# LayerNorm's small operations between statistics and power: from VectorE to GpSimd, in two-operand form

## The chip, the cores and the metric

The kernel runs on one core of a Trainium2 chip. The metric is the device time of one execution in microseconds (us). Three runs of the kernel before gave 407.63, 406.25 and 405.65 us; their median is 406.25 us. The engines are PE (TensorE, matmuls), DVE (VectorE), ACT (ScalarE), POOL (GpSimd) and SP (SyncE, which only issues transfers here).

## What is computed

There are 16 batches (B) of 512 tokens (T) with 256 features (D), and a context of 64 rows (K) per batch. Two cross-attentions follow each other.

```
layer 0:  q = rmsnorm(x) Wq^T, 16 heads of 16;  k, v from rmsnorm(ctx)
          token t looks at the context rows idx[t]-1, idx[t], idx[t]+1 only
          w = relu(q.k / 4)^2, divided by max(sum w, 1e-6);  x' = x + (w v) Wo^T
layer 1:  q = gelu(x' Wq + bq), k, v = gelu(ctx W + b), one head
          y = softmax(q k^T) v Wf + bf + x'
          out = (y - mean(y)) * rsqrt(var(y) + 1e-5) * gamma + beta     over the 256 features
```

The change concerns the last line alone. VectorE's `bn_stats` gives for every row of y the mean and the sum of squared deviations (m2) of its even and of its odd elements. With these, mean = (mean_e + mean_o) / 2 and var = (m2_e + m2_o) / D + (mean_e - mean_o)^2 / 4.

## The kernel before

All of it is written by hand: five instruction streams, one for each engine, with semaphores. Nothing is planned by a scheduler, and each stream is in order.

After a prologue for the weights and the context, a software pipeline runs over the batches. `steps` calls, for every engine, `step(f, b, n)`: the layer-0 attention of batch f, the layer-1 queries and softmax of batch b = f-1, and the end of batch n = f-2 (value product, LayerNorm, output). There is a step (0, -, -), a step (1, 0, -), then the steps from f=2 to f=14, the step of f=15 (`last`, in which no next batch is prepared), the step (-, 15, 14) and the step (-, -, 15). VectorE's step is cut in a `head` and a `tail` (`steps_turned`).

What stands around the change in a step, by engine and line:

- TensorE: picked keys (L388, a matmul with a one-hot matrix as look-up); L465, which adds the values of batch n to y in PSUM and signals `z_mm`; the output projection of b (L346 to L348); the first half of the next batch's layer-0 query product (L346 to L348, weight q0); the head sums (L495), which need the third key product (`qk_ready`) and signal `s_mm`; the second half of the query product; four transposes of the scores (L513), which need `s_cp`; the layer-1 queries of b (L346, weight q1), which need `xp_hi` and `xp_lo`; picked values (L394), which need `zn_ready` for the bank they write; then the turning of the attention output (L414), scores (L562, L570), and the softmax's transposes (L580).
- VectorE, `head`: two key products (L819), `bn_stats` of batch n (L834, four instructions, the last signals `stats_ready`), the six small operations (L839 to L846), the third key product (L819), the sum `xpT` (L861, from PSUM and the input), `xp_lo` (L864, from two SBUF tiles). `tail`: the row sum `den` (L883) and what follows from it, the three attention products (L870), the one-hot matrices, the softmax, `o_lo` (L927).
- GpSimd: `x_lo` of the next batch (L298), the power `rstd` = var^(-0.5) (L310), `nbias` = -mean * rstd (L313), then multiplication by gamma (L321), addition of beta (L323) and the output's transfer (L325).
- ScalarE: `normalise(range(0, 2))` (L666, y * rstd + nbias for two of the four row tiles; waits for `z_mm` and `nbias_ready`), `round_xp` (L687, `xp_hi`), the copy of the scores `s_sb` (L702, waits for `s_mm`), a copy of the next queries (L656), the square of the weights (L709, waits for TensorE's transposes), `normalise(range(2, 4))`, and the rest. In the step (-, 15, 14) `round_xp` stands ahead of the normalise. In the last step there is only the LayerNorm: statistics, power, normalise, gamma and beta on VectorE (L937, L939), output.

Of the kernel before, what the change touches and what calls it, by code (L numbers as in the profile page):

```python
# [5 lines left out]
B, T, D, K, H = 16, 512, 256, 64, 16  # L6
HD = D // H
P = 128
DC = D // P
TT = T // P  # L10
# [4 lines left out]
LN_EPS = 1e-05  # L15
# [7 lines left out]
def xattn_pair(nc: bass.Bass, xT, ctx, ctxT, idx, vectors, wq0T, wk0T, wv0T, wo0T,  # L23
# [4 lines left out]
    ALU = mybir.AluOpType  # L28
# [4 lines left out]
    with es:  # L33
        def sb(name, shape, dt=f32):
            return es.enter_context(nc.sbuf_tensor(name, shape, dt))
# [14 lines left out]
        minus_half = sb("minus_half", [P, CT])  # L50
# [39 lines left out]
        enf = sb("enf", [P, TT, K])  # L90
        eT = sb("eT", [P, 2, P])
        stats = sb("stats", [P, TT, 6])
        mean_gap, nmean2, m2_sum, gap_sq, var = (sb(n, [P, TT]) for n in ("mean_gap", "nmean2", "m2_sum", "gap_sq", "var"))
        rstd = sb("rstd", [P, TT])
        nmean = sb("nmean", [P, TT])
        nbias = sb("nbias", [P, TT])
        bufs = sb("bufs", [P, 8, DC * T])

# [5 lines left out]
        def rows(t):  # L104
# [38 lines left out]
        smax_ready, sdiff_ready, ex_ready, ssum_ready, rsum_ready, enf_ready = map(sem, (  # L143
            "smax_ready", "sdiff_ready", "ex_ready", "ssum_ready", "rsum_ready", "enf_ready"))
        eT_mm, eT_ready, z_mm = map(sem, ("eT_mm", "eT_ready", "z_mm"))
        stats_ready, parts_ready, gap_ready, var_ready, rstd_ready, nmean_ready, nbias_ready = map(sem, (
            "stats_ready", "parts_ready", "gap_ready", "var_ready", "rstd_ready", "nmean_ready", "nbias_ready"))
        zn_ready, zg_ready, zo_ready, out_done, last_zg, last_zo, last_out_done = map(sem, (
            "zn_ready", "zg_ready", "zo_ready", "out_done", "last_zg", "last_zo", "last_out_done"))

        def out_rows(j, at=0, cols=D):

            at += (j % 2) * D
            return ps[:, 6 + j // 2, at:at + cols]
# [12 lines left out]
        def steps(engine, step):  # L167
            step(0, None, None)
            step(1, 0, None)
            for i in range(FIRST_STEADY, LAST_STEADY):  # L170
                step(i, i - 1, i - 2)
            step(B - 1, B - 2, B - 3, last=True)
            step(None, B - 1, B - 2)
            step(None, None, B - 1)
# [17 lines left out]
        def first(n):  # L192
            return isinstance(n, int) and n == 0

        def is_last(n):
            return isinstance(n, int) and n == B - 1

        def f32_view(t):
            return t.bitcast(f32)
# [82 lines left out]
        @block.gpsimd  # L282
        def _(pool):
            G = nc.gpsimd
            G.memset(minus_half[:, :], -0.5).then_inc(half_set, 1)

            def context_scale(n):

                tiles = slice(4 * n, 4 * n + 4)
                pool.wait_ge(cms_done, 4 * n + 4)  # L290
                G.tensor_scalar(cmean[:, tiles], cms[:, tiles], 1.0 / D, EPS_RMS, ALU.mult, ALU.add).then_inc(cmean_done, 1)
                pool.wait_ge(cmean_done, n + 1)
                pool.wait_ge(half_set, 1)
                G.tensor_tensor(crs[:, tiles], cmean[:, tiles], minus_half[:, tiles], ALU.pow).then_inc(crs_done, 1)  # L294

            def split_x_lo(f):
                pool.wait_ge(xh_ready, 2 * f + 2)
                G.tensor_tensor(x_lo[:, :, :], x_ring[:, f % RING, :, :], f32_view(x_hi[:, :, :]), ALU.subtract).then_inc(xl_ready, 2)  # L298

            context_scale(0)  # L300
            split_x_lo(0)
            context_scale(1)

            def step(f, b, n, last=False):
                if f is not None and not last:
                    split_x_lo(f + 1)
                if n is not None:

                    pool.wait_ge(var_ready, n + 1)
                    G.tensor_tensor(rstd[:, :], var[:, :], minus_half[:, 0:TT], ALU.pow).then_inc(rstd_ready, 1)  # L310
                    pool.wait_ge(rstd_ready, n + 1)
                    pool.wait_ge(nmean_ready, n + 1)
                    G.tensor_tensor(nbias[:, :], nmean[:, :], rstd[:, :], ALU.mult).then_inc(nbias_ready, 1)  # L313
                if n is not None and not is_last(n):

                    pool.wait_ge(zn_ready, 2 * n + 2)
                    if first(n):
                        pool.wait_ge(ln_in, 16 * 2)
                    else:
                        pool.wait_ge(out_done, 16 * n)  # L320
                    G.tensor_tensor(zo, zn, lng_row[:, :].unsqueeze(1).broadcast_to([P, TT, D]), ALU.mult).then_inc(zg_ready, 1)  # L321
                    pool.wait_ge(zg_ready, n + 1)
                    G.tensor_tensor(zo, zo, lnb_row[:, :].unsqueeze(1).broadcast_to([P, TT, D]), ALU.add).then_inc(zo_ready, 1)  # L323
                    pool.wait_ge(zo_ready, n + 1)
                    pool.dma_start(out[n].rearrange("(j p) d -> p j d", p=P), zo).then_inc(out_done, 16)  # L325

            steps(pool, step)
            pool.wait_ge(out_done, 16 * (B - 1))

# [260 lines left out]
        def _(act):  # L590
# [79 lines left out]
            def step(f, b, n, last=False):  # L670
# [19 lines left out]
                    round_xp()  # L690
                if n is not None:
                    act.wait_ge(z_mm, n + 1)
                    act.wait_ge(nbias_ready, n + 1)
                    if not first(n):
                        act.wait_ge(zg_ready, n)
                    normalise(range(0, 2))
# [20 lines left out]
                if b is not None:  # L717
                    for e in range(DC):
# [3 lines left out]
                        i = A(q1T[:, e, :], ps[:, 2 + e, :], ACT.Gelu, bias=vec[:, 2, e:e + 1])  # L722
# [19 lines left out]
        def _(dve):  # L742
            V = nc.vector
# [77 lines left out]
            def head(f, b, n):  # L821
                if f is not None:
                    multiply_keys(f, 0, 4)
                    if first(f):
                        for t in range(4, 6):
                            keys_values_remainder(t)
                    multiply_keys(f, 1, 0)
                    if first(f):
                        for t in range(6, CT):
                            keys_values_remainder(t)  # L830
                if n is not None:
                    dve.wait_ge(z_mm, n + 1)
                    for j in range(TT):
                        i = V.bn_stats(stats[:, j, :], out_rows(j))  # L834
                    i.then_inc(stats_ready, 1)

                    dve.wait_ge(stats_ready, n + 1)
                    mean_e, m2_e, mean_o, m2_o = (stats[:, :, i] for i in (1, 2, 4, 5))
                    V.tensor_tensor(mean_gap[:, :], mean_e, mean_o, ALU.subtract)  # L839
                    V.scalar_tensor_tensor(nmean2[:, :], mean_e, -1.0, mean_o, ALU.mult, ALU.subtract)  # L840
                    V.scalar_tensor_tensor(m2_sum[:, :], m2_e, D * LN_EPS, m2_o, ALU.add, ALU.add).then_inc(parts_ready, 1)
                    dve.wait_ge(parts_ready, n + 1)
                    V.scalar_tensor_tensor(gap_sq[:, :], mean_gap[:, :], 0.25, mean_gap[:, :], ALU.mult, ALU.mult).then_inc(gap_ready, 1)
                    V.tensor_scalar(nmean[:, :], nmean2[:, :], 0.5, None, ALU.mult).then_inc(nmean_ready, 1)
                    dve.wait_ge(gap_ready, n + 1)
                    V.scalar_tensor_tensor(var[:, :], m2_sum[:, :], 1.0 / D, gap_sq[:, :], ALU.mult, ALU.add).then_inc(var_ready, 1)  # L846
                if f is not None:
                    multiply_keys(f, 2, 4)
                    if first(f):
                        dve.wait_ge(w1_in, 16 * 2)  # L850
                        for t in range(2, 6):
                            dve.wait_ge(kv_in[t], 32)
                        for i, name in enumerate(("o0", "q1")):
                            V.tensor_copy(w_hi[name][:, :, :], raw[name]).then_inc(w1_hi_ready, 1)
                            dve.wait_ge(w1_hi_ready, i + 1)
                            V.tensor_tensor(w_lo[name][:, :, :], raw[name], f32_view(w_hi[name][:, :, :]), ALU.subtract).then_inc(w1_ready, 1)
                if b is not None:

                    for g in range(DC):
                        dve.wait_ge(xp_mm, 2 * b + g + 1)  # L860
                        V.tensor_tensor(xpT[:, g, :], ps[:, 2 + g, :], x_ring[:, b % RING, g, :], ALU.add).then_inc(xp_ready, 1)  # L861
                    for g in range(DC):
                        dve.wait_ge(xph_ready, 2 * b + g + 1)
                        V.tensor_tensor(xp_lo[:, g, :], xpT[:, g, :], f32_view(xp_hi[:, g, :]), ALU.subtract).then_inc(xpl_ready, 1)  # L864
# [117 lines left out]
```

## Time and profile before

| | |
|---|---|
| median of 3 runs | 406.25 us (405.65 to 407.63) |
| profiled execution | 407.22 us, its span 405.4 us |
| mean granted TensorE clock | 0.98 |
| busy: PE, DVE, ACT, POOL | 91%, 76%, 57%, 37% of the span |
| one steady step (from one L298 on GpSimd to the next) | 209.88 to 231.13, 21.25 us |

The profile is of one execution. A line of the timeline is a run of like instructions with the time in which the engine stood idle before it and what ended that; "issue" there is a wait that the profile puts down to nothing. Busy time is an average over stages with different limits, so what a change is worth is read from the stage in which it stands. The profiled execution took 0.97 us more than the median.

### The profile page before, as it was taken

To read this page: it belongs to the slowest core of one execution; us is meant where nothing else is said; L and a number is where in the kernel's file an instruction comes from. 1 tells how busy PE (TensorE), PEld (TensorE's weight loads), DVE (VectorE), ACT (ScalarE), POOL (GpSimd) and SP (SyncE) were. 2 spreads that over 40 slices of the span, in tenths; PEclk is the share of its full clock that TensorE was granted. 3 is DMA by queue.
4 is the path that set the end of the run, shared out by engine and by line. 5 is a ranking of instruction groups with operands and counts; after the bars stand their busy time and mean duration, and the time that the engine had idled before them with its cause. 6 is when DMAs were issued, how large, how long until landed. Compare 5 with 4: busy or idle time off the path is not lost.

```text
span 405.4 us, 5734 instructions
## 1 busy us (share of the span) xinstructions
PE 370.7 (91%) x2132; PEld 262.5 (65%) x2132; DVE 306.2 (76%) x588; ACT 231.6 (57%) x379; POOL 148.8 (37%) x102
## 2 busy tenths in 40 slices
PE   3977999999999999999999999999999999998660
PEld 1653886858576776767676767676768576756540
DVE  0888266887979796969696969697978879797614
ACT  4793413557475656575656657474747474746441
POOL 0630002035353534434343525253535353515151
PEclk9998999999999999999999999999999999999985
DMA  8875056012011212121212121212121110010111
GB/s 253 282 214 158 0 128 159 0 54 64 32 72 43 78 53 78 53 79 54 78 54 78 53 78 53 78 52 81 52 77 54 41 68 25 0 53 11 41 53 52
DMA packets 17339, 30.24 MB, mean 75 GB/s; under 512 B 1568, under 2 KB 7712, under 8 KB 17312
## 3 DMA queue, kind: packets, MB, share of 16 engines
q1 hardware_dynamic: 14192, 21.22, 17.3%
q0 software_dynamic: 2160, 7.87, 5.5%
q10 hardware_dynamic: 960, 0.79, 0.6%
q8 instruction: 17, 0.28, 0.3%
q14 instruction: 10, 0.08, 0.1%
HBM read 17.29 MB, written 8.39 MB: 63 GB/s over the span
## 4 chain that ended last, share of the span: by engine, by line
PE 80%; issue 7%; ACT 5%; DVE 4%; POOL 3%; ACTq 0%; POOLq 0%; DVEq 0%
PE ps L346 11%; PE ps L348 10%; PE ps L347 10%; PE ps L414 10%; PE ps L495 7%; PE ps L394 7%; PE ps L388 6%; PE ps L465 4%; PE ps L562 4%; PE ps L550 3%; PE ps L513 2%; PE ps L378 2%; PE ps L580 1%; PE ps L570 1%; POOL crs L294 1%
## 5 line engine op out<-in xcount | busy, mean ns | idle before, releaser
L298 POOL TENSOR_TENSOR x_lo<-x_ring,x_hi 128x1024 fp32r<-128x1024 f32 x16 | 38.4, 2401 | 104.5 <-ACT x_hi L642 104.5
L666 ACT ACTIVATE bufs<-ps,nbias,rstd 128x256 f32<-128x256 f32 x64 | 32.3, 561 | 65.6 <-issue 55.6
L321 POOL TENSOR_TENSOR bufs<-bufs,lng_row 128x1024 f32<-128x1024 f32 x15 | 35.9, 2396 | 87.5 <-ACT bufs L666 87.5
L870 DVE TENSOR_TENSOR qkp<-ps,wn 128x1024 f32<-128x1024 f32 x48 | 57.3, 1221 | 6.2 <-PE ps L394 4.9
L819 DVE TENSOR_TENSOR qkp<-ps,bufs 128x1024 f32<-128x1024 f32 x48 | 57.1, 1217 | 0.1
L414 PE MATMUL ps<-cst,qkp 128*128 128x128 f32 x384 | 50.3, 275 | 0.0
L414 PEld LDWEIGHTS ps<-cst,qkp 128*128 128x128 f32 x384 | 42.5, 140 | 5.9 <-DVE qkp L870 5.8
L388 PE MATMUL ps<-onehot,kv 128*128 128x512 f32 x96 | 33.9, 436 | 6.5 <-issue 4.8
L323 POOL TENSOR_TENSOR bufs<-bufs,lnb_row 128x1024 f32<-128x1024 f32 x15 | 35.7, 2378 | 1.2
L883 DVE TENSOR_REDUCE den<-ps 128x64 f32<-128x192 f32 x16 | 5.7, 358 | 40.2 <-ACT ps L709 40.2
L495 PE MATMUL ps<-qkp,cst 128*32 128x512 f32 x192 | 32.0, 621 | 2.2 <-DVE qkp L819 2.2
L394 PE MATMUL ps<-kv,onehot 128*128 128x256 f32 x192 | 33.1, 299 | 0.2 <-DVE wn L892 0.2
L394 PEld LDWEIGHTS ps<-kv,onehot 128*128 128x128 f32 x192 | 27.0, 189 | 9.4 <-ACT bufs L666 5.2
L495 PE MATMUL ps<-bufs,cst 128*32 128x512 f32 x64 | 31.8, 621 | 0.0
L310 POOL TENSOR_TENSOR rstd<-var,minus_half 128x4 f32<-128x4 f32 x16 | 16.5, 1029 | 37.3 <-DVE var L846 37.3
L864 DVE TENSOR_TENSOR xp_lo<-bufs,xp_hi 128x512 fp32r<-128x512 f32 x32 | 20.9, 689 | 10.1 <-ACT xp_hi L687 10.0
L346 PE MATMUL ps<-xp_hi,wh_q 128*128 128x512 f32 x64 | 26.4, 412 | 2.3 <-DVE xp_lo L864 2.3
L722 ACT ACTIVATE bufs<-ps,vec 128x512 f32<-128x512 f32 x32 | 22.1, 690 | 9.3 <-PE ps L348 9.1
L346 PE MATMUL ps<-x_hi,wh_q 128*128 128x512 f32 x64 | 27.1, 423 | 0.0
L388 PEld LDWEIGHTS ps<-onehot,kv 128*128 128x128 f32 x96 | 14.5, 189 | 18.1 <-issue 15.1
L834 DVE BATCH_NORM_STATS2 stats<-ps 128x6 f32<-128x256 f32 x64 | 22.7, 419 | 4.4 <-PE ps L465 4.4
L348 PE MATMUL ps<-xp_lo,wh_q 128*128 128x512 f32 x64 | 25.3, 395 | 0.0
(137 smaller groups left out, 831.7 us busy)
## 6 DMA issues: line engine op xcount, KB each, us to landing
x_ring<-xT SPq DMA_DIRECT2D x16, 512.0 KB, 3.5
out<-bufs POOLq DMA_DIRECT2D x15, 512.0 KB, 3.4
idx_ring<-idx SPq DMA_DIRECT2D x16, 256.0 KB, 3.7
vfd<-bufs SPq DMA_DIRECT2D x8, 256.0 KB, 5.3
qkp<-ctxT SPq DMA_DIRECT2D x2, 512.0 KB, 7.5
bufs<-ctx SPq DMA_DIRECT2D x2, 512.0 KB, 8.9
kv<-kv_cross SPq DMA_DIRECT2D x8, 128.0 KB, 2.4
out<-bufs SPq DMA_DIRECT2D x2, 256.0 KB, 2.2
```

The costliest lines, as they stand in the source:

```text
L298: G.tensor_tensor(x_lo[:, :, :], x_ring[:, f % RING, :, :], f32_view(x_hi[:, :, :]), ALU.subtract).then_inc(xl_ready, 2)
L321: G.tensor_tensor(zo, zn, lng_row[:, :].unsqueeze(1).broadcast_to([P, TT, D]), ALU.mult).then_inc(zg_ready, 1)
L323: G.tensor_tensor(zo, zo, lnb_row[:, :].unsqueeze(1).broadcast_to([P, TT, D]), ALU.add).then_inc(zo_ready, 1)
L346: mm(o, hi, m_hi, start=start, stop=False)
L347: mm(o, lo, m_hi, start=False, stop=False)
L348: last = mm(o, hi, m_lo, start=False, stop=stop)
L388: i = mm(ps[:, bank0 + g, :], kv0[:, f, 0, g * P:(g + 1) * P], onehot[:, s, :], start=True, stop=True)
L394: i = mm(ps[:, bank0 + j // 2, (j % 2) * D:(j % 2 + 1) * D], onehot[:, s, j * P:(j + 1) * P], kv0[:, f, 1, :], start=True, stop=True)
L414: i = mm(ps[:, g, j * P:(j + 1) * P], att[:, s, j, g * P:(g + 1) * P], ident, is_transpose=True, start=(s == 0 and j == 0), stop=(s == SHI ...
L495: i = mm(ps[32 * s:32 * s + 32, 4, :], sum_sel[:, g if s < SHIFTS else 2, :], qk[:, s, g, :] if s < SHIFTS else xsq[:, g, :], start=(g == ...
L819: V.tensor_tensor(qk[:, s, :, :], ps[:, bank0:bank0 + 2, :], q0, ALU.mult).then_inc(qk_ready, 1)
L870: V.tensor_tensor(att[:, s, :, :].rearrange("p j (h d) -> p (j h) d", d=HD), ps[:, bank0:bank0 + 2, :].rearrange("p a (h d) -> p (a h) d", ...
```

## The change

The six small operations leave VectorE's stream. GpSimd's stream does the same arithmetic behind `stats_ready`, without the three-operand form (`scalar_tensor_tensor`), which makes more of them: it works with four times the variance, takes the power of that (which gives half of 1/sigma), and doubles it. GpSimd had two instructions here and now has ten. Each pair that depends on the other has a semaphore between. ScalarE waits for `nbias_ready` twice as far, as rstd and nbias each signal it. Four tiles of 128x4 are added and two removed.

```diff
@@ gpsimd, step
-                    pool.wait_ge(var_ready, n + 1)
-                    G.tensor_tensor(rstd[:, :], var[:, :], minus_half[:, 0:TT], ALU.pow).then_inc(rstd_ready, 1)
+                    pool.wait_ge(stats_ready, n + 1)
+                    mean_e, m2_e, mean_o, m2_o = (stats[:, :, i] for i in (1, 2, 4, 5))
+                    G.tensor_tensor(mean_gap[:, :], mean_e, mean_o, ALU.subtract).then_inc(gap_ready, 1)
+                    G.tensor_tensor(m2_sum[:, :], m2_e, m2_o, ALU.add).then_inc(parts_ready, 1)
+                    pool.wait_ge(gap_ready, 2 * n + 1)
+                    G.tensor_tensor(gap_sq[:, :], mean_gap[:, :], mean_gap[:, :], ALU.mult).then_inc(gap_ready, 1)
+                    pool.wait_ge(parts_ready, n + 1)
+                    G.tensor_scalar(m2_part[:, :], m2_sum[:, :], 4.0 / D, 4.0 * LN_EPS, ALU.mult, ALU.add).then_inc(var_ready, 1)
+                    G.tensor_tensor(mean2[:, :], mean_e, mean_o, ALU.add).then_inc(mean_ready, 1)
+                    pool.wait_ge(gap_ready, 2 * n + 2)
+                    pool.wait_ge(var_ready, 2 * n + 1)
+                    G.tensor_tensor(var4[:, :], m2_part[:, :], gap_sq[:, :], ALU.add).then_inc(var_ready, 1)
+                    pool.wait_ge(mean_ready, 2 * n + 1)
+                    G.tensor_scalar(nmean2[:, :], mean2[:, :], -1.0, None, ALU.mult).then_inc(mean_ready, 1)
+                    pool.wait_ge(var_ready, 2 * n + 2)
+                    G.tensor_tensor(half_rstd[:, :], var4[:, :], minus_half[:, 0:TT], ALU.pow).then_inc(rstd_ready, 1)
                     pool.wait_ge(rstd_ready, n + 1)
-                    pool.wait_ge(nmean_ready, n + 1)
-                    G.tensor_tensor(nbias[:, :], nmean[:, :], rstd[:, :], ALU.mult).then_inc(nbias_ready, 1)
+                    pool.wait_ge(mean_ready, 2 * n + 2)
+                    G.tensor_tensor(rstd[:, :], half_rstd[:, :], half_rstd[:, :], ALU.add).then_inc(nbias_ready, 1)
+                    G.tensor_tensor(nbias[:, :], nmean2[:, :], half_rstd[:, :], ALU.mult).then_inc(nbias_ready, 1)
@@ scalar, step
-                    act.wait_ge(nbias_ready, n + 1)
+                    act.wait_ge(nbias_ready, 2 * n + 2)
@@ vector, head
-                    dve.wait_ge(stats_ready, n + 1)
-                    mean_e, m2_e, mean_o, m2_o = (stats[:, :, i] for i in (1, 2, 4, 5))
-                    V.tensor_tensor(mean_gap[:, :], mean_e, mean_o, ALU.subtract)
-                    V.scalar_tensor_tensor(nmean2[:, :], mean_e, -1.0, mean_o, ALU.mult, ALU.subtract)
-                    V.scalar_tensor_tensor(m2_sum[:, :], m2_e, D * LN_EPS, m2_o, ALU.add, ALU.add).then_inc(parts_ready, 1)
-                    dve.wait_ge(parts_ready, n + 1)
-                    V.scalar_tensor_tensor(gap_sq[:, :], mean_gap[:, :], 0.25, mean_gap[:, :], ALU.mult, ALU.mult).then_inc(gap_ready, 1)
-                    V.tensor_scalar(nmean[:, :], nmean2[:, :], 0.5, None, ALU.mult).then_inc(nmean_ready, 1)
-                    dve.wait_ge(gap_ready, n + 1)
-                    V.scalar_tensor_tensor(var[:, :], m2_sum[:, :], 1.0 / D, gap_sq[:, :], ALU.mult, ALU.add).then_inc(var_ready, 1)
```

## Rows read from the trace of the kernel before

**Rows 1.** The page's busy line: engine, busy us (share of the span), instructions.
```profile
PE 370.7 (91%) x2132; PEld 262.5 (65%) x2132; DVE 306.2 (76%) x588; ACT 231.6 (57%) x379; POOL 148.8 (37%) x102
```

**Rows 2.** Timeline, a steady step: start, duration (us), engine, line, operation, count, [idle before].
```profile
209.16 0.70 PE L388 MATMUL ps<-onehot,kv 128*128 128x512 f32 x2 [0.34 <-issue]
...
209.88 2.38 POOL L298 TENSOR_TENSOR x_lo<-x_ring,x_hi 128x1024 fp32r<-128x1024 f32 x1 [4.20 <-ACT x_hi L642]
...
211.24 1.42 DVE L834 BATCH_NORM_STATS2 stats<-ps 128x6 f32<-128x256 f32 x4
...
212.69 0.17 DVE L839 TENSOR_TENSOR mean_gap<-stats 128x4 f32<-128x4 f32 x1
...
213.32 1.22 DVE L819 TENSOR_TENSOR qkp<-ps,bufs 128x1024 f32<-128x1024 f32 x1
213.48 1.03 POOL L310 TENSOR_TENSOR rstd<-var,minus_half 128x4 f32<-128x4 f32 x1 [1.22 <-DVE var L846]
...
214.59 0.20 POOL L313 TENSOR_TENSOR nbias<-nmean,rstd 128x4 f32<-128x4 f32 x1
...
214.87 1.02 ACT L666 ACTIVATE bufs<-ps,nbias,rstd 128x256 f32<-128x256 f32 x2 [4.20 <-issue]
...
215.66 0.63 PE L495 MATMUL ps<-qkp,cst 128*32 128x512 f32 x3
...
216.44 1.29 DVE L864 TENSOR_TENSOR xp_lo<-bufs,xp_hi 128x512 fp32r<-128x512 f32 x2 [0.71 <-ACT xp_hi L687]
...
217.65 0.69 ACT L702 ACTIVATE s_sb<-ps,cst 128x512 f32<-128x512 f32 x1 [0.72 <-PE ps L495]
...
218.80 0.59 PEld L513 LDWEIGHTS ps<-cst,s_sb 128*128 128x128 f32 x4
...
219.36 0.19 PEld L346 LDWEIGHTS ps<-xp_hi,wh_q 128*128 128x128 f32 x1
...
220.02 0.36 DVE L883 TENSOR_REDUCE den<-ps 128x64 f32<-128x192 f32 x1 [2.28 <-ACT ps L709]
```

**Rows 3.** Timeline, the prologue: GpSimd's small instructions, and VectorE beside the second.
```profile
10.55 0.35 POOL L291 TENSOR_SCALAR cmean<-cms 128x4 f32<-128x4 f32 x1 [9.72 <-ACT scT L611]
...
10.99 4.02 POOL L294 TENSOR_TENSOR crs<-cmean,minus_half 128x4 f32<-128x4 f32 x1
...
14.98 2.73 POOL L298 TENSOR_TENSOR x_lo<-x_ring,x_hi 128x1024 fp32r<-128x1024 f32 x1
...
20.97 1.23 DVE L748 TENSOR_TENSOR xp_lo<-qkp,xp_hi 128x1024 fp32r<-128x1024 f32 x1
...
21.11 1.14 POOL L291 TENSOR_SCALAR cmean<-cms 128x4 f32<-128x4 f32 x1 [3.40 <-ACT scT L611]
```

**Rows 4.** Timeline, the step of batch 15 in f.
```profile
363.22 0.63 PE L495 MATMUL ps<-qkp,cst 128*32 128x512 f32 x3 [0.26 <-DVE qkp L819]
...
363.51 1.02 ACT L666 ACTIVATE bufs<-ps,nbias,rstd 128x256 f32<-128x256 f32 x2 [5.15 <-issue]
...
366.19 0.66 PE L513 MATMUL ps<-cst,s_sb 128*128 128x128 f32 x4 [1.05 <-ACT s_sb L702]
```

**Rows 5.** Timeline, the step (-, 15, 14).
```profile
378.81 1.42 DVE L834 BATCH_NORM_STATS2 stats<-ps 128x6 f32<-128x256 f32 x4 [1.27 <-PE ps L465]
...
382.36 1.47 DVE L864 TENSOR_TENSOR xp_lo<-bufs,xp_hi 128x512 fp32r<-128x512 f32 x2
...
383.01 1.92 ACT L666 ACTIVATE bufs<-ps,nbias,rstd 128x256 f32<-128x256 f32 x4
...
387.74 1.08 PE L562 MATMUL ps<-bufs,k1T 128*64 128x256 f32 x8 [0.78 <-ACT bufs L722]
```

**Rows 6.** Timeline, the last step (-, -, 15).
```profile
395.32 1.43 DVE L834 BATCH_NORM_STATS2 stats<-ps 128x6 f32<-128x256 f32 x4 [3.09 <-PE ps L465]
...
398.97 1.93 ACT L666 ACTIVATE bufs<-ps,nbias,rstd 128x256 f32<-128x256 f32 x4 [5.82 <-POOL nbias L313]
```

More of the change, by code:

```diff
@@ L92, in xattn_pair @@
         stats = sb("stats", [P, TT, 6])
-        mean_gap, nmean2, m2_sum, gap_sq, var = (sb(n, [P, TT]) for n in ("mean_gap", "nmean2", "m2_sum", "gap_sq", "var"))
+        mean_gap, mean2, nmean2, m2_sum, m2_part, gap_sq, var4, half_rstd = (sb(n, [P, TT]) for n in (
+            "mean_gap", "mean2", "nmean2", "m2_sum", "m2_part", "gap_sq", "var4", "half_rstd"))
         rstd = sb("rstd", [P, TT])
-        nmean = sb("nmean", [P, TT])
         nbias = sb("nbias", [P, TT])
@@ L145, in xattn_pair @@
         eT_mm, eT_ready, z_mm = map(sem, ("eT_mm", "eT_ready", "z_mm"))
-        stats_ready, parts_ready, gap_ready, var_ready, rstd_ready, nmean_ready, nbias_ready = map(sem, (
-            "stats_ready", "parts_ready", "gap_ready", "var_ready", "rstd_ready", "nmean_ready", "nbias_ready"))
+        stats_ready, parts_ready, gap_ready, mean_ready, var_ready, rstd_ready, nbias_ready = map(sem, (
+            "stats_ready", "parts_ready", "gap_ready", "mean_ready", "var_ready", "rstd_ready", "nbias_ready"))
         zn_ready, zg_ready, zo_ready, out_done, last_zg, last_zo, last_out_done = map(sem, (
```

## The prediction, made before the changed kernel ran

> **What bounds the kernel now.** I read the page's busy line first, then the timeline of one steady step, then the last three steps. TensorE is busy for 91% of the span and VectorE for 76% [rows 1], so VectorE is not full, and GpSimd least of all. In the steady step VectorE stands idle for 2.28 us in front of the row sum of the weights, waiting for ScalarE's square of them, which waits for TensorE [rows 2]. So what VectorE saves earlier in the step is given back there. TensorE itself hardly stops: its one clear pause in the step is 0.34 us in front of the first look-up of keys [rows 2].
>
> The change touches one path: the end of the statistics (`bn_stats`), the small operations, the power, `nbias`, and ScalarE's `normalise(0..2)`. ScalarE's stream is in order, so behind that normalise stand the two roundings of xp (`xp_hi`), then the copy of the scores `s_sb`. For the former waits VectorE's `xp_lo` and then TensorE's second query product; for the latter wait TensorE's four transposes (L513).
>
> Times of the steady step [rows 2]: the statistics end at 211.24 + 1.42 = 212.66. Six small VectorE instructions run from 212.69 until the third key product starts at 213.32, so they cost 0.63 us. The power starts at 213.48 (1.03 us), `nbias` at 214.59 (0.20 us), the normalise at 214.87. From the end of the statistics to the normalise it is 2.21 us. The same interval in the last step is 398.97 - (395.32 + 1.43) = 2.22 us [rows 6].
>
> **Part 1, VectorE gives up six instructions a step.** 16 steps by 0.63 us are 10 us of busy time. Their worth: the third product would end at 213.9 and not at 214.54, but TensorE only gets to its consumer (L495) at 215.66 behind two products, so it was already 1.1 us early. The sum `xpT` would come up to 0.5 us earlier, but ScalarE takes it up only behind the normalise. In the step with the last element there is no next query product as cover, and TensorE does wait 0.26 us for the third product [rows 4]; but the wait that comes after, 1.05 us for `s_sb`, ends on ScalarE's chain and swallows it. I take 0 for part 1. Bounds: 0, and 0.26 us gained once.
>
> **Part 2, GpSimd runs nine small instructions beside the power, where it ran one.** GpSimd is free for it: `x_lo` ends at 209.88 + 2.38 = 212.26, before the statistics [rows 2]. The new waits are GpSimd's on itself and one on the statistics; queued behind them is the scaling of the output, which waits for the second normalise anyway, so nobody else is kept. What counts is by how much later than 2.21 us the normalise starts; call that d. From rows: a 128x4 two-input operation takes 0.20 us (`nbias`); a GpSimd instruction that waits for the one before it starts 0.08 us behind its end (214.51 to 214.59), and ScalarE also 0.08 us behind `nbias` [rows 2]. One that waits for nothing started 0.03 us before its forerunner's end (power 10.99 + 4.02 = 15.01, `x_lo` at 14.98) [rows 3], so 0.17 us behind the start of one of 0.20. A hot tensor_scalar of this size is not seen alone: its two rows are 0.35 and 1.14 us, both with VectorE working on SBUF beside it [rows 3]; I take 0.25, between `nbias` and the shorter.
>
> Counted from the end of the statistics: mean_gap 0.09 to 0.29; m2_sum 0.26 to 0.46; gap_sq 0.43 to 0.63; m2_part 0.60 to 0.85; mean2 0.82; var4 0.99 to 1.19; nmean2 1.16 to 1.41; power 1.38 to 2.41; rstd 2.49 to 2.69; nbias 2.66 to 2.86; normalise at 2.94. So d = 2.94 - 2.21 = 0.73 us. Lower bound: independent instructions 0.08 us apart (VectorE's own, as close as the dependent gap) and a tensor_scalar of 0.20: then dependencies alone set the pace, the power starts at 1.01, the normalise at 2.48, d = 0.27. Upper bound: no overlap at all, 0.28 us per two-input operation and 0.43 per tensor_scalar: the power starts at 0.09 + 5 x 0.28 + 2 x 0.43 = 2.35, the normalise at 4.02, d = 1.81. I stay with 0.73, since the spacing has a row.
>
> **What hides it in the 13 steady steps.** ScalarE idles 0.72 us in front of `s_sb` for TensorE's sums, and `s_sb` ends at 217.65 + 0.69 = 218.34, where TensorE's transposes start only at 218.80, with 0.05 us for the signal [rows 2]. So 0.72 + 0.41 = 1.13 us of d is free. The other branch has more: `xp_lo` ends at 216.44 + 1.29 = 217.73 and its product starts at 219.36, 1.6 us later. With d = 0.73 the cost is 0 in each of the 13; beyond 1.13 it is 13 x (d - 1.13).
>
> **The last three steps have no such cover.** (a) Step of the last element (normalise at 363.51): TensorE waits 1.05 us for `s_sb`, which follows the normalise and both roundings without a gap [rows 4]. All of d counts: +0.73. (b) The step after it: the roundings stand ahead of the normalise, so the start at 383.01 is ScalarE's own; `nbias` was ready 2.22 us behind 380.23, at 382.45, so 0.56 us is free, and 0.17 is left of d. But here VectorE's `xp_lo` (both inputs in SBUF) runs from 382.36 to 383.83 [rows 5], just when rstd (382.72) and nbias would read SBUF. At 21.11 a GpSimd instruction started while such a VectorE instruction ran from 20.97 to 22.20, and it ended at 22.25 [rows 3]: it was held to the end. Held behind both halves of `xp_lo`, nbias lands at about 383.9, and the normalise starts at about 384.0 in place of 383.01, +1.0. Between 0.17 and 1.0 I take 0.9, nearer the row of the held instruction. TensorE's next product waits there for ScalarE (0.78 us) [rows 5], so it counts. (c) The last step is one chain from the statistics to the output: +0.73 [rows 6].
>
> The Trainium skill, SBUF — State Buffer, Who interferes with whom, says that a VectorE instruction with two SBUF inputs contends with a GpSimd one that reads SBUF, and that the second to issue blocks. By that rule the power, if it started first, could also hold `xp_lo`; the trace agrees on the other order (1.14 us against 0.35), and without the rule (b) would be 0.17.
>
> **Sum.** 0.73 + 0.9 + 0.73 = 2.4 us. The profiled execution took 407.22 us (span 405.4 and 1.8 around it), so it would take 409.6; it was 1.0 us above the median of 406.25, and on the median's footing the forecast is 408.6 us, +0.6%. What a measurement of this kernel can tell from no change is about 0.5%, 2.0 us, so the forecast lies close to that border.
>
> **Rivals.** *Short chain.* GpSimd overlaps its small instructions better than 0.17 us apart and nbias slips in between the halves of `xp_lo`: d = 0.3, 0.3 + 0.1 + 0.3 = 0.7 us, 407.0. For it: VectorE's like instructions (L839 on) do start 0.08 us apart. Against it: the only GpSimd row of a pair without a wait shows 0.03 us of overlap. *The cover breaks.* If each of the small instructions costs its span and the gap, 0.28 us, the power starts at 2.05, the normalise at 3.72, d = 1.51, over the 1.13 that are free. The place is ScalarE's `s_sb` in each steady step: 13 x 0.38 = 4.9, and with 1.5, 1.0 and 1.5 at the end 8.9 us, 415.2; at the upper bound d = 1.81 it is 8.8 + 1.8 + 1.3 + 1.8 = 13.7, 420. Against it is the 14.98 row; for it, that no row shows eight short GpSimd instructions in a row, and that the tensor_scalar is unmeasured. The Trainium skill, Perfetto Trace Analysis, GPSIMD Engine Instruction, calls a GpSimd span unreliable and wants start-to-start spacing; by it the 0.20 may leave out work ahead of the start, which is this rival's mechanism; no run here shows it so far. *Faster.* VectorE's 0.63 us reaches the end of its step, where TensorE pauses 0.34 us for `o_lo` before the look-up: 13 x 0.34 = 4.4 us gained, less 2.4, 404.2. Its place is the tail of VectorE's step; it decides if VectorE has a backlog from the products to `o_lo`. Against it: the 2.28 us of idle time in between [rows 2]. *It does nothing:* the change would have to leave the normalise's start where it is (d near 0), which ten instructions where two stood exclude, short of 0.27.
>
> **How the numbers follow.** Forecast (d 0.5 to 1.1, all in the last three steps, +1.5 to +3.4) 0.60; short chain 0.20; cover breaks 0.15; faster 0.05. The range of 406.7 to 413.0 holds the forecast, most of the short chain and the start of the broken cover, where d lies between 1.13 and 1.4. Of the forecast's 0.60, some 0.38 lies above the border at 408.3; with 0.15 that is 0.53 slower. Same is 0.22 + 0.20 less a little for noise, 0.42; faster 0.05.
>
> **What would show it.** Right: a steady step of the same length (21.2 us from one `x_lo` to the next), ScalarE's idle time before `s_sb` cut from 0.72 us to near 0 with TensorE's L513 where it was, the normalise 2.9 us behind the statistics, VectorE's wait before the row sum up by 0.6 us, and the last normalise 2.9 us behind its statistics. Part (b) is right if nbias ends after 383.8 less the shift of (a). The cover is broken if TensorE's L513 waits for `s_sb` in steady steps. The prediction is wrong if the step's length changes, or if d is under 0.4 or over 1.1.

## The result, and the profile after

The changed kernel took 408.16 us (median of 7 runs, 407.62 to 409.92), the kernel before 405.84 us (7 runs, 405.63 to 407.67): ratio 1.0052, 95% interval 1.0027 to 1.0078. Twelve more runs gave 1.0051 (1.0028 to 1.0074). It is slower by 2.1 us by the ratio and 2.3 by the medians, and both intervals lie above 1; the forecast was 408.6 and +2.4.

The two profiled executions (407.22 us before, 408.79 after) can't simply be subtracted. The one before had a stretch with TensorE at half its clock in the prologue, the one after had it near the end. Besides, TensorE is at half its clock over the last 12 us and more of both (from 393.0 before, from 394.5 after), 2.3 and 1.5 us of it ahead of the last product. The table by stretches shows the first two; its columns are the stretch, its length, then busy us (and instructions) of PE, PEld, DVE, ACT and POOL, the granted clock (1.00 is 2.4 GHz, 0.50 is 1.2 GHz), the share of the DMA engines and GB/s. Before:

```profile
38.00:42.00 4.00, 4.00 (x20) 1.52 (x13) 1.57 (x3) 1.15 (x2) 0.00 (x0) 0.58 0.18 41
...
384.00:388.00 4.00, 3.22 (x14) 2.32 (x16) 0.00 (x0) 3.59 (x6) 2.92 (x2) 1.00 0.01 4
```

The changed kernel:

```profile
38.00:42.00 4.00, 4.00 (x27) 2.40 (x20) 1.63 (x3) 1.86 (x3) 0.00 (x0) 1.00 0.19 45
384.00:388.00 4.00, 3.98 (x11) 2.71 (x9) 0.00 (x0) 2.66 (x4) 3.15 (x2) 0.57 0.02 4
```

So I compare inside stages, from the start of one instruction to that of another. Busy time of the changed kernel: VectorE lost 9.7 us, GpSimd gained 22.3 [rows 1].

```profile
PE 370.3 (91%) x2132; PEld 262.3 (64%) x2132; DVE 296.5 (73%) x492; ACT 230.7 (57%) x379; POOL 171.1 (42%) x230
```

A steady step of the changed kernel, from its timeline; it answers to [rows 2]. The trace leaves the digits out of names: m_part is m2_part, mean is mean2, var is var4, nmean is nmean2.

```profile
208.41 2.38 POOL L298 TENSOR_TENSOR x_lo<-x_ring,x_hi 128x1024 fp32r<-128x1024 f32 x1 [4.15 <-ACT x_hi L657]
...
209.77 1.42 DVE L849 BATCH_NORM_STATS2 stats<-ps 128x6 f32<-128x256 f32 x4
...
211.10 1.21 DVE L834 TENSOR_TENSOR qkp<-ps,bufs 128x1024 f32<-128x1024 f32 x1
...
211.27 0.21 POOL L311 TENSOR_TENSOR mean_gap<-stats 128x4 f32<-128x4 f32 x1 [0.47 <-DVE stats L849]
...
211.43 0.21 POOL L312 TENSOR_TENSOR m_sum<-stats 128x4 f32<-128x4 f32 x1
...
211.58 0.20 POOL L314 TENSOR_TENSOR gap_sq<-mean_gap 128x4 f32<-128x4 f32 x1
...
211.87 0.19 POOL L316 TENSOR_SCALAR m_part<-m_sum 128x4 f32<-128x4 f32 x1
...
212.14 0.20 POOL L317 TENSOR_TENSOR mean<-stats 128x4 f32<-128x4 f32 x1
...
212.65 1.03 POOL L324 TENSOR_TENSOR half_rstd<-var,minus_half 128x4 f32<-128x4 f32 x1
...
214.19 1.02 ACT L681 ACTIVATE bufs<-ps,nbias,rstd 128x256 f32<-128x256 f32 x2 [4.99 <-issue]
...
215.76 1.29 DVE L868 TENSOR_TENSOR xp_lo<-bufs,xp_hi 128x512 fp32r<-128x512 f32 x2 [2.17 <-ACT xp_hi L702]
...
216.15 0.69 ACT L717 ACTIVATE s_sb<-ps,cst 128x512 f32<-128x512 f32 x1
...
218.51 0.36 DVE L887 TENSOR_REDUCE den<-ps 128x64 f32<-128x192 f32 x1 [1.45 <-ACT ps L724]
```

The statistics end at 211.19 and the normalise starts at 214.19, 3.00 us later, 2.21 before: d = 0.79 us. ScalarE no longer idles before `s_sb` (0.72 us before). The freed time of VectorE is waiting time elsewhere: its wait before `xp_lo` rose from 0.71 to 2.17 us and the one before the row sum fell from 2.28 to 1.45, together 0.63 us more, which is what the six instructions took. The step is as long as it was: twelve of them, from the `x_lo` at 80.90 to the one at 335.84, take 254.94 us, and 254.81 before (82.48 to 337.29).

The last three steps, first the line of the kernel before from which its (a) is measured, then the changed kernel's timeline [rows 4 to 6]:

```profile
359.87 1.42 DVE L834 BATCH_NORM_STATS2 stats<-ps 128x6 f32<-128x256 f32 x4
```

```profile
358.48 1.41 DVE L849 BATCH_NORM_STATS2 stats<-ps 128x6 f32<-128x256 f32 x4
...
365.58 0.66 PE L528 MATMUL ps<-cst,s_sb 128*128 128x128 f32 x4 [2.18 <-ACT s_sb L717]
...
378.20 1.43 DVE L849 BATCH_NORM_STATS2 stats<-ps 128x6 f32<-128x256 f32 x4 [1.27 <-PE ps L480]
...
381.79 1.47 DVE L868 TENSOR_TENSOR xp_lo<-bufs,xp_hi 128x512 fp32r<-128x512 f32 x2
...
382.20 0.33 POOL L327 TENSOR_TENSOR rstd<-half_rstd 128x4 f32<-128x4 f32 x1
382.49 0.19 POOL L328 TENSOR_TENSOR nbias<-nmean,half_rstd 128x4 f32<-128x4 f32 x1
382.76 1.93 ACT L681 ACTIVATE bufs<-ps,nbias,rstd 128x256 f32<-128x256 f32 x4 [0.23 <-POOL nbias L328]
...
388.75 1.08 PE L577 MATMUL ps<-bufs,k1T 128*64 128x256 f32 x8 [0.78 <-ACT bufs L737]
...
396.09 1.43 DVE L849 BATCH_NORM_STATS2 stats<-ps 128x6 f32<-128x256 f32 x4 [2.83 <-PE ps L480]
...
400.51 1.93 ACT L681 ACTIVATE bufs<-ps,nbias,rstd 128x256 f32<-128x256 f32 x4 [6.35 <-POOL nbias L328]
```

(a) Statistics to the transposes (L513, now L528): 7.10 us, before 366.19 - 359.87 = 6.32: +0.78. (c) End of the last statistics to the last normalise: 2.99, before 2.22: +0.77. (b) Statistics to the scores (L562, now L577): 10.55, before 387.74 - 378.81 = 8.93; but here lay the half-clock stretch. It began during the second query product and let TensorE finish it at about 388, so it is no measure of (b). The next run's profile had none at that place.

### The profile page after: what moved, and what is told of

Its sections match the earlier page's. It is cut to its first block and busy times, and to the rows that moved or that the text cites. A ratio compares the mean times of both kernels' runs of the same rounds, so it can differ in the third digit from the quotient of the medians.

```text
span 407.0 us, 5782 instructions
## 1 busy us (share of the span) xinstructions
PE 370.3 (91%) x2132; PEld 262.3 (64%) x2132; DVE 296.5 (73%) x492; ACT 230.7 (57%) x379; POOL 171.1 (42%) x230
## 5 line engine op out<-in xcount | busy, mean ns | idle before, releaser
L510 PE MATMUL ps<-qkp,cst 128*32 128x512 f32 x192 | 30.7, 598 | 1.9 <-DVE qkp L834 1.9
L510 PE MATMUL ps<-bufs,cst 128*32 128x512 f32 x64 | 30.5, 598 | 0.0
L403 PEld LDWEIGHTS ps<-onehot,kv 128*128 128x128 f32 x96 | 14.5, 189 | 18.1 <-issue 15.1
L362 PE MATMUL ps<-xp_hi,wl_q 128*128 128x512 f32 x64 | 25.9, 404 | 0.0
```

The costliest lines, as they stand in the source:

```text
L362: mm(o, lo, m_hi, start=False, stop=False)
L403: i = mm(ps[:, bank0 + g, :], kv0[:, f, 0, g * P:(g + 1) * P], onehot[:, s, :], start=True, stop=True)
L510: i = mm(ps[32 * s:32 * s + 32, 4, :], sum_sel[:, g if s < SHIFTS else 2, :], qk[:, s, g, :] if s < SHIFTS else xsq[:, g, :], start=(g == ...
```

## The experiments

Each is an edit of the changed kernel. In the runs that mix the two forms, VectorE's form has semaphores of its own. The kernels with a ratio were timed in turn with the kernel before on one chip; ratios of different experiments can be of different chips. Where one time stands alone, there was one execution.

**The changed kernel again.** No edit.

> The changed kernel once more, beside the next ones. Theory (all of the loss lies in the last three steps): 1.0055 of the kernel before, about +2.2 us; in its profile the normalise starts 3.0 us behind the statistics in every step. TensorE's clock at 1.2 GHz in the second query product of the step (-, 15, 14), which the first profile of the changed kernel showed, is by the theory 'chance of that execution' absent here or seen as often in other variants; by the rival 'the longer wait for s_sb brings it' it is there again.

Measured: 408.65 against 406.90 us, 1.0051 (1.0028 to 1.0074). Its step (-, 15, 14) has no half-clock stretch:

```profile
382.54 1.43 DVE L849 BATCH_NORM_STATS2 stats<-ps 128x6 f32<-128x256 f32 x4 [1.27 <-PE ps L480]
...
390.31 1.26 ACT L737 ACTIVATE bufs<-ps,vec 128x512 f32<-128x512 f32 x2
...
391.63 1.08 PE L577 MATMUL ps<-bufs,k1T 128*64 128x256 f32 x8 [0.92 <-ACT bufs L737]
```

The statistics start at 382.54, the scores at 391.63, 9.09 us, so (b) is +0.16. This execution had three half-clock stretches, at 38, 62 and 369 us, the last one behind the wait for `s_sb`; so the one at 384 was not bound to its place.

**VectorE in the last three, and the complement.** The branch is `if n < 13` (GpSimd's form) in the first and `if n >= 13` in the second.

```diff
+                  if on_pool(n):       # n < 13, or n >= 13
                       ... the ten instructions
+                  else:
+                      pool.wait_ge(v_var_ready, k + 1)
+                      G.tensor_tensor(rstd[:, :], var[:, :], minus_half[:, 0:TT], ALU.pow).then_inc(rstd_ready, 1)
...
+                      G.tensor_tensor(nbias[:, :], nmean[:, :], rstd[:, :], ALU.mult).then_inc(nbias_ready, 2)
```

> GpSimd does the small operations for batches 0 to 12, VectorE (as before) for 13, 14 and 15. Theory (13 steady steps cost nothing, the loss is in the last three): the time of the kernel before, within 0.3 us. Rival (the steady steps lose a little each, 0.1 to 0.2 us): 1.3 to 2.3 us above it.

> The complement: VectorE for batches 0 to 12, GpSimd for 13, 14 and 15. Theory: all of the loss, the time of the changed kernel, +2.2 us on the kernel before. Rival (the steady steps carry it): within 0.5 us of the kernel before.

Measured: 406.06 us, 0.9997 (0.9980 to 1.0014), with VectorE in the last three, and 409.65 us, 1.0066 (1.0036 to 1.0096), with GpSimd there alone. Thirteen of the sixteen moves cost nothing that these runs can show (0.6 us at most, by the interval), and twelve steady steps of that kernel are as long as before; the other three make the loss. In the second kernel's profile (a) is 7.12 us and (b) 9.09. By the ratio the first is within the 0.3 us that I had given; by the medians it lies 0.8 us below.

**How much cover a steady step has.** Two or six more additions on GpSimd, for batches 0 to 12.

```diff
+                    for r in range(6 if n < 13 else 0):     # 2 in the other kernel
+                        G.tensor_tensor(pad[:, r, :], mean2[:, :], mean2[:, :], ALU.add)
                     pool.wait_ge(var_ready, 2 * n + 2)
                     G.tensor_tensor(half_rstd[:, :], var4[:, :], minus_half[:, 0:TT], ALU.pow).then_inc(rstd_ready, 1)
```

> The changed kernel with six more 128x4 additions on GpSimd ahead of the power, for batches 0 to 12 only. In a row they should start 0.155 us apart, so d rises from 0.79 to 1.72 us. Theory (1.13 us of d are free in a steady step, at ScalarE's copy of the scores): 13 x (1.72 - 1.13) = +7.7 us on the changed kernel, and TensorE's four transposes wait for s_sb in each steady step. Rival (ScalarE has more room than I counted, so steady steps still cost nothing): +0 us. Rival (no room left at all): 13 x 0.93 = +12 us.

> The changed kernel with two more 128x4 additions on GpSimd ahead of the power, for batches 0 to 12 only: d rises from 0.79 to 1.10 us in a steady step. Theory, mended by the run with six: a steady step has 1.37 us of d free (0.72 and 0.41 as predicted, and 0.23 more, because only the weight load of the transposes, not the matmul, came at the earlier time), so two cost nothing: steady step 21.2 us, time that of the changed kernel. Rival (each small instruction on GpSimd costs the step something, 0.32 / 6 us each): 13 x 0.11 = +1.4 us.

Six: 413.84 us, 1.0168 (1.0142 to 1.0193), 4.8 us over the changed kernel and not 7.7. Its timeline:

```profile
211.74 2.38 POOL L299 TENSOR_TENSOR x_lo<-x_ring,x_hi 128x1024 fp32r<-128x1024 f32 x1 [4.17 <-ACT x_hi L660]
...
213.10 1.42 DVE L852 BATCH_NORM_STATS2 stats<-ps 128x6 f32<-128x256 f32 x4
...
218.42 1.02 ACT L684 ACTIVATE bufs<-ps,nbias,rstd 128x256 f32<-128x256 f32 x2 [5.88 <-issue]
...
220.37 0.69 ACT L720 ACTIVATE s_sb<-ps,cst 128x512 f32<-128x512 f32 x1
...
221.11 0.66 PE L531 MATMUL ps<-cst,s_sb 128*128 128x128 f32 x4
...
233.28 2.37 POOL L299 TENSOR_TENSOR x_lo<-x_ring,x_hi 128x1024 fp32r<-128x1024 f32 x1 [4.14 <-ACT x_hi L660]
```

Here the normalise is 3.90 us behind the statistics, d = 1.69. The transposes start 0.05 us behind `s_sb`, so they wait for it, and the step takes 21.54 us. Twelve steps take 258.52 us (82.44 to 340.96), 254.94 in the changed kernel: 0.30 more each, 3.9 us for 13. The mechanism was right, the price half (of the 4.8 us the steps account for 3.9; the rest is within the interval): the room is 1.69 - 0.30 = 1.39 us, not 1.13. I had measured it to the weight load of the transposes (218.80 in [rows 2]); their first matmul comes only 0.23 us later. Two: the normalise is 3.32 us behind the statistics (d = 1.11), and twelve steps take 254.94 us (82.28 to 337.22), as in the changed kernel. Timed 408.79 us, 1.0065 (1.0039 to 1.0090), which overlaps the changed kernel's interval and alone would not exclude the 1.4 us of the rival; the length of the steps does.

**Does a VectorE instruction with two SBUF inputs hold GpSimd?** Two additions for batch 14 alone (`if n == 14`).

> The changed kernel with two more 128x4 additions ahead of the power for batch 14 alone (step (-, 15, 14)). They move nbias 0.31 us later, out of the gap between the two halves of xp_lo into the second half. Theory (a VectorE instruction with two SBUF inputs holds a GpSimd read to its end): nbias takes about 0.65 us and not 0.19, and the normalise starts 3.7 us behind the statistics (3.1 without the additions). Rival (no holding; the 0.30 us of rstd has another reason): nbias stays at 0.19 us, the normalise at 3.4 us.

```profile
381.57 1.47 DVE L871 TENSOR_TENSOR xp_lo<-bufs,xp_hi 128x512 fp32r<-128x512 f32 x2
...
382.29 0.20 POOL L330 TENSOR_TENSOR rstd<-half_rstd 128x4 f32<-128x4 f32 x1
382.43 0.66 POOL L331 TENSOR_TENSOR nbias<-nmean,half_rstd 128x4 f32<-128x4 f32 x1
383.18 1.93 ACT L684 ACTIVATE bufs<-ps,nbias,rstd 128x256 f32<-128x256 f32 x4 [0.86 <-POOL nbias L331]
```

As the theory has it: rstd, which now starts in the gap between the halves (382.25 to 382.35), takes 0.20 us, and nbias, which meets the second half (it ends at 383.04), takes 0.66 us and ends at 383.09. The normalise is 3.76 us behind the statistics. One execution, 408.68 us; it had a half-clock stretch at 384.

**The order of GpSimd's instructions.** mean2 moved ahead of gap_sq, nmean2 ahead of m2_part.

> The same ten instructions of GpSimd in another order: mean2 and nmean2 ahead of gap_sq's neighbour m2_part. In the changed kernel m2_part starts 0.28 us behind gap_sq and mean2 0.27 us behind m2_part, where the other pairs are 0.155 us apart. Theory A (the cost is the two-operation tensor_scalar's own, 0.12 us ahead of it and 0.12 behind): the 0.28 and 0.27 stay at m2_part, d stays at 0.79. Theory B (the gaps are signals that come late in this order): they shrink or move to other instructions and d falls by 0.1 to 0.25 us.

The timeline of its GpSimd:

```profile
214.06 0.20 POOL L315 TENSOR_TENSOR gap_sq<-mean_gap 128x4 f32<-128x4 f32 x1
214.22 0.23 POOL L317 TENSOR_SCALAR nmean<-mean 128x4 f32<-128x4 f32 x1
214.53 0.19 POOL L319 TENSOR_SCALAR m_part<-m_sum 128x4 f32<-128x4 f32 x1
214.87 0.20 POOL L322 TENSOR_TENSOR var<-m_part,gap_sq 128x4 f32<-128x4 f32 x1
215.15 1.04 POOL L324 TENSOR_TENSOR half_rstd<-var,minus_half 128x4 f32<-128x4 f32 x1
```

The gaps stay at m_part, 0.31 us ahead of it and 0.34 behind; that is theory A. But d did not stay at 0.79, it rose to 0.97 (3.18 us), because in this order var4 and the power each wait for the instruction right before them. Neither theory had that. Why this tensor_scalar takes longer than the other (0.155 us behind var4 in the changed kernel) stays open. One execution, 411.23 us, with three half-clock stretches.

**ScalarE's roundings ahead of the normalise** in the step of batch 15 in f, and then, in another kernel, `s_sb` as well, with VectorE's form for batches 14 and 15.

```diff
-                if b is not None and f is None:
+                if b is not None and (f is None or last):
                     round_xp()
+                if last:
+                    copy_scores()        # the second kernel only: the wait for s_mm, and s_sb
```

> The changed kernel with one more change in the step of batch 15 in f alone: ScalarE rounds xp ahead of the first two normalises, not behind them. Theory (in that step the chain statistics, GpSimd, normalise, rounding, s_sb delays TensorE's four transposes): the roundings now lie in the time in which GpSimd works, s_sb comes about 0.9 us earlier, and the whole by as much, -0.5 to -0.9 us on the changed kernel. If xp_lo, now at the same time as rstd and nbias, holds them back, it is 0.3 to 0.6. Rival (the loss of that step lies elsewhere): 0.

> GpSimd does the small operations for batches 0 to 13, VectorE for 14 and 15; and in the step of batch 15 in f ScalarE does the roundings and s_sb ahead of the first two normalises. Theory: steps (-, 15, 14) and (-, -, 15) as in the kernel before, and the transposes some 5.8 us behind the start of the statistics, 6.3 before: 0.3 to 0.5 us less than the kernel before, 405.7 where that has 406.1. Rival (the loss was elsewhere): 1 to 2 us above the kernel before.

The first kernel's `xp_lo` and rstd in that step:

```profile
362.47 1.44 DVE L868 TENSOR_TENSOR xp_lo<-bufs,xp_hi 128x512 fp32r<-128x512 f32 x2
362.62 0.60 POOL L327 TENSOR_TENSOR rstd<-half_rstd 128x4 f32<-128x4 f32 x1
```

The first: statistics at 358.64, transposes at 365.11, 6.47 us and not 7.10, so 0.63 of the 0.78 is won back, and rstd was held by the first half of `xp_lo` (0.60 us) as feared. Timed 407.51 us, 1.0047 (1.0021 to 1.0073): too near to the changed kernel's 1.0051 to show 0.6 us. The second: 5.74 us in the profile (360.01 to 365.75), 6.32 before, as forecast; timed 406.73 us, 1.0007 (0.9983 to 1.0031), the kernel before and not less, so this forecast missed. What the stage won, 0.58 us, is smaller than the interval; and its profile shows another loss, at the end: from the issue of the last output transfer (401.60) to the end of the span it is 3.34 us, 2.57 in the kernel before. An 8 KB packet of the trace's kind "instruction" ran for 0.43 us inside that transfer. The profile of the third kernel of the next experiment, which has the same form, shows the same (3.33 us, a packet of 0.51 us); the other twelve have 2.49 to 2.57 us and no such packet. Whether the packet makes the delay was not tested, but a loss of 0.77 us there would hide the gain.

**TensorE kept busy in its waits.** Unused matmuls into a free PSUM bank: six in the wait for `s_sb`; then also eight in the wait for `xp_lo` of the step (-, 15, 14); then three and eight in the kernel with `s_sb` first.

```diff
+                    for r in range(6 if last else 0):
+                        mm(ps[:, 0, :], w_hi["q0"][:, 0, 0:P], x_hi[:, 0, :], start=True, stop=True)
                     pe.wait_ge(s_cp, f + 1)
```

> The changed kernel with six more matmuls (128x128 by 512, into a PSUM bank that is free there, their result unused) where TensorE waits 2.2 us for s_sb in the step of batch 15 in f. They fit into the wait (6 x 0.23 = 1.4 us), so the chain is as long as before. Theory (the longer wait brings 3 to 4 us of TensorE at 1.2 GHz behind it, seen in the last three steps of 6 of 8 profiles with GpSimd there and in none of the 2 with VectorE there): no such stretch behind L528 in the profile, mean clock of the runs up, 0.3 to 0.6 us less than the changed kernel. Rival (the stretches come whatever stands there): the time of the changed kernel, stretches as often.

> As the run before, and eight more such matmuls in TensorE's 2.3 us wait for xp_lo in the step (-, 15, 14). Theory: neither of the two places has a stretch at 1.2 GHz, 0.5 to 1.0 us less than the changed kernel (so 1.2 to 1.7 us above the kernel before: the chain itself, 0.78 + 0.16 + 0.77 = 1.7). Rival (whatever stands there): the time of the changed kernel.

> As the run before, with three unused matmuls in the wait for s_sb and eight in the wait for xp_lo. Theory: 0.3 to 0.5 us less for the order and up to 0.5 less for the clock, 0.998 of the kernel before. Rival: no different from the run without them.

One wait filled: 410.26 us, 1.0086 (1.0056 to 1.0117), if anything worse; its profile had no half-clock stretch behind the filled wait, but one behind the other wait (0.66 in the row). The theory failed for this run. Both filled: 407.82 us, 1.0033 (1.0007 to 1.0059), no stretch in the profile up to the last product. That is 1.3 us over the kernel before, in the range of the forecast, but its interval overlaps the changed kernel's. The rows are of the stretch behind the second wait in the kernel with one filled, and of the last three steps in the kernel with both:

```profile
385.00:390.00 5.00, 4.55 (x12) 3.13 (x12) 0.00 (x0) 3.64 (x6) 3.59 (x2) 0.66 0.01 3
```

```profile
360.00:394.00 34.00, 28.62 (x170) 19.90 (x168) 17.74 (x32) 18.29 (x30) 16.50 (x26) 1.00 0.09 31
```

The third kernel: 406.68 us, 1.0007 (0.9985 to 1.0029), no different from the one without matmuls; the forecast of 0.998 missed.

The clock of the timed runs says more than single profiles. The mean granted clock was 0.9821, 0.9831 and 0.9829 for the kernel before (24, 18 and 30 runs), 0.9822 with VectorE in the last three (12 runs), and 0.9818 with `s_sb` first, with and without matmuls (12 each). With GpSimd in the last three it was 0.9804 and 0.9789 (7 and 12, the changed kernel), 0.9786 (7) in the complement, 0.9786 (5) and 0.9772 (4) with two and six additions, 0.9800 (12) with the roundings first, 0.9767 (7) with one wait filled, and 0.9829 (12) with both filled. Most of these means are good to about 0.001. Within the 24 runs of the kernel before, each us at 1.2 GHz goes with 0.37 us of time. The changed kernel's 12 runs had 2.7 us more at 1.2 GHz than the 24 beside them (17.2 against 14.5, from 2 x (1 - clock) x span); about 0.8 of it is the longer end, in which TensorE has nothing to do, and the rest would be 0.7 us. An estimate from this, the chain of 1.7 us (below) and 0.37 us for each further us at 1.2 GHz, gives 2.4 us for the changed kernel, 2.5 for the complement, 3.3 with one wait filled and 1.4 with both; by the ratios they took 2.1, 2.7, 3.5 and 1.3.

## Why the prediction was right

*Part 1, nothing for VectorE's freed time.* Right in the timelines: the step kept its length, and 13 moves together gave 0.9997. Also in the step of the last element: the 0.26 us wait for the third product went, and the wait for `s_sb` grew from 1.05 to 2.18 us. One sign named for it failed: the wait before the row sum was to grow by 0.6 us and fell by 0.83. The time is given back earlier, before `xp_lo`, because ScalarE's `xp_hi` comes later by d.

*d = 0.73 us.* Measured 0.79. The spacing of 0.17 us was 0.155, and a tensor_scalar takes 0.19 to 0.23 us, not 0.25; two places have 0.28 us between starts. The errors nearly cancel.

*The cover of 1.13 us.* It is 1.39. The forecast did not depend on it; the rival "the cover breaks" did, and would have been too dear by 0.26 us a step.

*(a) +0.73:* measured 0.78. *(c) +0.73:* 0.77.

*(b) +0.9: wrong in size.* The mis-sized term is nbias held behind both halves of `xp_lo`, and by its own sign (nbias ending after 383.8 less the shift) it failed: nbias ended at 382.68. Holding is real, as batch 14 with two additions shows (0.66 us) and the kernel with the roundings first (0.60 us), but rstd was held behind the first half only, and nbias slipped into the gap: the normalise came 0.35 us later against its statistics (3.13 and 2.78). And of that only 0.16 reached the scores. The two gelus behind it took 1.44 us before (386.24 to 387.68), as the second waited for TensorE's product, and 1.26 us in the changed kernel's second profile, where they started 0.34 us later against the statistics and had no wait. I had let all of ScalarE's delay count. The line of the kernel before:

```profile
386.24 1.44 ACT L722 ACTIVATE bufs<-ps,vec 128x512 f32<-128x512 f32 x2
```

So the chain makes 0.78 + 0.16 + 0.77 = 1.7 us. What brings it near the measured 2.1 to 2.3 is, most likely, a term I did not have: TensorE spends more time at 1.2 GHz in the kernels with GpSimd in the last three steps, some 0.5 to 0.7 us. That it goes with these steps is what the mean clocks of the mixed kernels say (0.9822 and 0.9786). That the longer wait for `s_sb` is its cause is not shown: filling that wait alone did not bring it back, filling both waits did, and the second wait is as long in the kernel before (2.26 us in both). This stays open. So does where in the steps the time at 1.2 GHz is added: single profiles don't tell, since the last half-clock stretch also starts at changing places. In the kernel before it began 2.3 us ahead of the last product and in the one with both waits filled behind it, and from the statistics of batch 14 to those of batch 15 it took them 16.51 and 15.76 us; but the kernel with `s_sb` first and no matmuls took 15.56. The total of 2.4 us was therefore partly luck: 0.7 too much in (b), 0.6 too little in the clock.

The rivals: the short chain is excluded by d, though its point that nbias slips in between the halves of `xp_lo` came true; the broken cover by the step's length; the faster one by that length too, and by the 1.45 us of idle time that are left before the row sum.

## What to carry to other kernels

A chain moved to a slower engine is free where something else ends later; here that held in 13 of 16 steps with 1.39 us of room, and all of the loss lay in the drain of the pipeline, where the same chain stands alone. So look up the last iterations separately, and give them the short form: VectorE for the last three gives the time before, though nothing less. Measure a cover to the instruction that does the work, not to the weight load ahead of it, and follow a delay past its first waiter before counting it.

## What the runs showed of the hardware

- GpSimd operations of 128x4 that wait for nothing start 0.155 us apart in the changed kernel, each taking 0.20 us; the power takes 1.03. The tensor_scalar with two operations is an exception: 0.27 to 0.34 us to its neighbours' starts.
- A GpSimd operation of 0.20 us took 0.66 us when it met a VectorE tensor_tensor with both inputs in SBUF, ending 0.05 us behind it. The power, which had started before, ran its 1.03 us beside it. The Trainium skill, SBUF — State Buffer, Who interferes with whom, has a VectorE instruction with two SBUF inputs contend with a GpSimd one that reads SBUF, and issue order decide which of them blocks; the trace agrees for the short operations, while `xp_lo`, issued during the power (381.09 to 382.12), ran at its usual 1.47 us for both halves, as in [rows 5], so the power did not hold it.
- Half-clock stretches of TensorE of 3 to 4 us came at changing places: at 384 us in one profiled execution of the changed kernel, at 38, 62 and 369 us in the other, beside the one at the very end that all fourteen profiles have. Profiles of two kernels should be compared stage by stage.
